# The first two tiles of a gated MLP block by column blocks, with loads reordered, part buffers doubled and the down weight rounded on another engine

## The reference

```
scale = cond @ norm_w.T + 1.0                       # (32, 256)
h = x * (scale[:, None, :] * rsqrt(mean(x*x) + 1e-6))
u = h @ up_w.T                                      # (.., 2048)
val, gate = split(u, 2)
h = val * gelu(gate)
hq = act_quant(h)      # per token: round(h * 127/max|h|) / (127/max|h|)
wq = weight_quant(down_w)   # ternary, by the mean of |down_w|
y = hq @ wq.T
return y + x
```

## Time and profile before

| | before |
|---|---|
| median of 3 runs (lowest to highest) | 429.09 us (429.09 to 429.58) |
| the profiled execution | 429.27 us |
| its span (first to last instruction) | 427.5 us |
| PE busy | 421.1 us, 99% of the span |
| DVE busy | 280.4 us, 66% |
| ACT busy | 186.4 us, 44% |
| POOL busy | 179.9 us, 42% |
| PE's share of the chain that ended last | 94% |

### The profile page before, as it was taken

How to read it: one execution, slowest core, us unless ns; L and a number is a source line. 1 busy time by engine, 2 the same in 40 slices (tenths; PEclk the granted TensorE clock), 3 DMA queues, 4 the chain that set the end, 5 groups by cost and what they waited for, 6 DMA issues and landing times.

```text
span 427.5 us, 7667 instructions
## 1 busy us (share of the span) xinstructions
PE 421.1 (99%) x2081; PEld 337.6 (79%) x2081; DVE 280.4 (66%) x539; ACT 186.4 (44%) x334; POOL 179.9 (42%) x323
## 2 busy tenths in 40 slices
PE   7999999999999999999999999999999999999997
PEld 5688888888887888887888888888878888878786
DVE  4987567556577566576565675565675665765676
ACT  5753444443444444444434444434444434444441
POOL 1564435435345344354344354353453353553520
PEclk9999999999999999999999999999999999999999
DMA  8434443334444334434244433343443344342324
GB/s 281 147 80 115 100 118 103 75 97 123 98 105 115 71 100 106 115 98 107 74 114 98 120 100 77 94 123 98 108 113 73 98 111 109 98 108 75 87 51 124
DMA packets 82024, 45.01 MB, mean 105 GB/s; under 512 B 68256, under 2 KB 68704, under 8 KB 81888
## 3 DMA queue, kind: packets, MB, share of 16 engines
q1 hardware_dynamic: 81584, 44.33, 39.8%
q10 hardware_dynamic: 432, 0.59, 0.4%
HBM read 20.00 MB, written 8.39 MB: 66 GB/s over the span
## 4 chain that ended last, share of the span: by engine, by line
PE 94%; DMA 1%; DVE 1%; SPq 1%; POOL 1%; issue 1%; ACT 0%; DVEq 0%; POOLq 0%
PE p_gate L678 41%; PE p_val L678 41%; PE p_y L698 12%; DMA up_raw<-up_w_t 1%; SPq L219 1%; DVE y_sb L500 0%; PE p_val L650 0%; POOL a_hi L311 0%; POOL scaled L308 0%; PE p_gate L650 0%; DVE q_rounded L526 0%; DVE h L547 0%; PE p_gate L657 0%; POOL a_lo L315 0%; DVE last_max L509 0%
## 5 line engine op out<-in xcount | busy, mean ns | idle before, releaser
L547 DVE SCALAR_TENSOR_TENSOR h<-p_val,rstd,gelu 128x512 f32<-128x512 f32 x128 | 95.3, 746 | 129.9 <-PE p_val L678 129.5
L389 ACT ACTIVATE gelu<-p_gate,rstd 128x512 f32<-128x512 f32 x128 | 87.5, 684 | 149.1 <-PE p_gate L678 139.4
L304 POOL TENSOR_TENSOR mean_sq_eps<-mean_sq,rms_eps 128x1 f32<-128x1 f32 x64 | 12.2, 190 | 224.3 <-PE p_val L678 210.3
L361 ACT ACTIVATE q<-q_rounded 128x1024 bf16<-128x1024 f32 x63 | 66.7, 1058 | 78.2 <-DVE q_rounded L582 78.2
L678 PE MATMUL p_gate<-up_hi,a_lo 128*128 128x512 f32 x248 | 80.6, 406 | 0.6 <-POOL a_lo L315 0.6
L678 PE MATMUL p_val<-up_hi,a_hi 128*128 128x512 f32 x248 | 78.2, 396 | 0.0
L678 PE MATMUL p_val<-up_hi,a_lo 128*128 128x512 f32 x248 | 78.1, 396 | 0.0
L678 PE MATMUL p_val<-up_lo,a_hi 128*128 128x512 f32 x248 | 78.1, 396 | 0.0
L678 PE MATMUL p_gate<-up_lo,a_hi 128*128 128x512 f32 x248 | 78.1, 395 | 0.0
L678 PE MATMUL p_gate<-up_hi,a_hi 128*128 128x512 f32 x248 | 78.1, 395 | 0.0
L568 DVE TENSOR_REDUCE h_max<-h 128x1 f32<-128x1024 f32 x63 | 76.6, 1216 | 1.2
(11 more groups left out here) (74 smaller groups left out, 247.1 us busy)
## 6 DMA issues: line engine op xcount, KB each, us to landing
xt_in<-x_t SPq DMA_DIRECT2D x32, 256.0 KB, 2.8
x_all<-x SPq DMA_DIRECT2D x32, 256.0 KB, 2.9
out<-y_sb SPq DMA_DIRECT2D x31, 256.0 KB, 2.0
up_raw<-up_w_t SPq DMA_DIRECT2D x6, 256.0 KB, 5.4
down_raw<-down_w_t SPq DMA_DIRECT2D x1, 1024.0 KB, 8.0
q_t<-q SPq DMA_TRANSPOSE x63, 3.1
up_raw<-up_w_t ACTq DMA_DIRECT2D x2, 256.0 KB, 3.1
out<-y_sb SPq DMA_DIRECT2D x1, 128.0 KB, 2.0
```

Source lines behind the costliest of these rows:

```text
L304: pool.tensor_tensor(mean_sq_eps[:, j:j + 1], mean_sq[:, j:j + 1], rms_eps[:, :], ALU.add).then_inc(pool_step, 1)
L361: act.activation(q[j % 2][:, :], q_rounded[j % 2][:, :], ACT.Copy, bias=-ROUND).then_inc(q_ready, 1)
L389: act.activation(gelu[c][:, :], p_gate[c][:, :], ACT.Gelu, scale=rstd[:, j:j + 1]).then_inc(gelu_done, 1)
L547: nc.vector.scalar_tensor_tensor(h[s][:, c * W:(c + 1) * W], p_val[c][:, :], rstd[:, j:j + 1], gelu[c][:, :], op0=ALU.mult, op1=ALU.mult). ...
```

## The change

Of the first two tiles, block c = 0 of tile 0, block 0 of tile 1, block 1 of tile 0 and block 1 of tile 1 are made in this order (`early_up`), tile t using the banks `p_gate[t]`, `p_val[t]`. Within a bank the order is a_hi and a_lo for k = 0, a_hi and a_lo for k = 1, then the two up_lo products. All loads go through SP, in a new order. POOL makes tile 1's parts, first of all its tiles; `a_hi` and `a_lo` have four buffers each, and from unit 1 on POOL's work for tile t waits for the values of tile t-3. `scale` is made in two halves in two banks. The down weight: |down_w| later in ACT's queue; the sum over partitions on PE, `ternary(0)` and `ternary(1)` on DVE in tile 2; one pass clips both ways, and the subtraction of `ROUND` with the conversion to bf16 is a copy on ACT (in tile 2, before the square for tile 4). The dummy tile holds ones, and three more dummy matmuls run first.

```diff
-        a_hi = [sb(f"a_hi{i}", [P, KD, P], fp32r) for i in range(2)]
-        a_lo = [sb(f"a_lo{i}", [P, KD, P], fp32r) for i in range(2)]
+        a_hi = [sb(f"a_hi{i}", [P, KD, P], fp32r) for i in range(UNIT)]
+        a_lo = [sb(f"a_lo{i}", [P, KD, P], fp32r) for i in range(UNIT)]
...
+        def early(t, c):
+
+            return t + TPB * c
...
             sp.dma_start(cond_norm_sb[:, :], cond_norm).then_inc(cond_norm_in, 16)
-            load_xt(0, 0)
-            load_up(1)
-            load_up(2)
-            load_x(0, 0)
-            load_up(3)
+            load_up(0, 0)
+            load_xt(0, 0)
+            load_up(0, 1)
+            load_up(1, 0)
+            load_up(1, 1)
+            load_x(0, 0)
+            for c in (2, 3):
+                for k in range(KD):
+                    load_up(c, k)
+            load_xt(0, 1)
             sp.dma_start(down_raw[:, :, :], down_w_t).then_inc(down_in, 16)
-            load_xt(0, 1)
             load_x(0, 1)
...
+            pool.wait_ge(xt_landed[0], 16)
+            product(0, 1)
+            low_part(1, 5)
+            mean(0, 0)
+            root(0, 6)
+            mean(1, 1)
+            root(1, 7)
+            for j in range(TPB, UNIT):
+                if j % TPB == 0:
+                    pool.wait_ge(xt_landed[j // TPB], 16)
+                product(0, j)
+                low_part(j, BEFORE + PER_TILE * (j - 2) + 2)
+                mean(j, j)
+                root(j, BEFORE + PER_TILE * (j - 2) + 3)
+
+            with pool.Fori(1, UNITS) as u:
                 for j in range(UNIT):
...
+                    pool.wait_ge(val_done, NP * (t - 2))
+                    mean(t, j)
+                    product(u, j)
+                    low_part(j, step + 3)
+                    root(j, step + 3)
...
-            for k in range(KD):
-                act.dma_start(up_raw[:, 0, k, :], up_w_t[0, 0, :, k, :]).then_inc(up_in[k], 16)
...
+            for c in range(2):
                 for k in range(KD):
...
+                    high_part(c, k)
+            square(0, 0, True)
+            square(0, 1, True)
+            high_part(2, 0)
+            early_gelu(0, 0)
+            high_part(2, 1)
+            high_part(3, 0)
+            high_part(3, 1)
+            early_gelu(1, 0)
+            early_gelu(0, 1)
+            act.wait_ge(down_in, 16)
+            act.activation(down_tmp[:, :, :], down_raw[:, :, :], ACT.Abs, accum_out=abs_sum[:, :]).then_inc(abs_ready, 1)
+            square(0, 2)
+            early_gelu(1, 1)
+            integers(0, 0, True)
+            square(0, 3)
...
+                    if first and j == TPB:
+
+                        act.wait_ge(ternary_step, 4)
+                        act.activation(down_t[:, :, :], down_tmp[:, :, :], ACT.Copy, bias=-ROUND).then_inc(down_ready, 1)
 
                     if j + 2 < UNIT:
                         square(u, j + 2)
...
-                    nc.vector.tensor_scalar(down_tmp[:, :, :], down_tmp[:, :, :], ROUND, 1.0,
-                                            ALU.subtract, ALU.min).then_inc(ternary_step, 1)
-                if stage == 2:
-
-                    dve.wait_ge(ternary_step, 4)
-                    nc.vector.tensor_scalar(down_t[:, :, :], down_tmp[:, :, :], -1.0, None,
-                                            ALU.max).then_inc(down_ready, 1)
+                    nc.vector.tensor_scalar(down_tmp[:, :, :], down_tmp[:, :, :], ROUND + 1.0, ROUND - 1.0,
+                                            ALU.min, ALU.max).then_inc(ternary_step, 1)
...
+            for c in range(2):
+                for k in range(KD):
+                    low_part(c, k)
+            low_part(2, 0)
+            early_h(0, 0)
+            low_part(2, 1)
+            low_part(3, 0)
+            low_part(3, 1)
+            early_h(1, 0)
+            early_h(0, 1)
+            quantised(0, 0, 0)
+            early_h(1, 1)
+            quantised(0, 1, 1)
+
             def unit(u, first, last=False):
-                for j in range(UNIT):
+                for j in range(TPB if first else 0, UNIT):
...
-                        if first and j == 1 and c == 0:
-                            ternary(1)
+                        if first and j == TPB:
+                            ternary(c)
+                        if first and j == TPB and c == 0:
+                            for done in range(TPB):
+                                rescale(0, done)
...
-            keep_busy(7)
+            keep_busy(10)
...
+            def early_up(t, c):
+
+                n = early(t, c)
+                if t == 1 and c == 0:
+
+                    pe.wait_ge(a_ready, 1)
+                for which, bank, done, read in ((0, p_gate[t], gate_done, gelu_done), (1, p_val[t], val_done, h_done)):
+                    col = 2 * c + which
+                    if c:
+
+                        pe.wait_ge(read, n - 1)
                     for k in range(KD):
...
+                        if t == 0 and c == 0 and which == 0:
+                            pe.wait_ge(a_hi_ready, k + 1)
+                        if t == 0:
+
+                            pe.wait_ge(up_hi_ready, col * KD + k + 1)
+                        nc.tensor.matmul(bank[:, :], a_hi[t][:, k, :], up_hi[:, col, k, :], start=(k == 0), stop=False)
+                        if t == 0 and n == 0 and which == 0 and k == 0:
+                            pe.wait_ge(first_a_ready, 1)
+                        nc.tensor.matmul(bank[:, :], a_lo[t][:, k, :], up_hi[:, col, k, :], start=False, stop=False)
+                    for k in range(KD):
+                        if t == 0:
 
                             pe.wait_ge(up_lo_ready, col * KD + k + 1)
...
+            for c in range(NP):
+                for t in range(TPB):
+                    early_up(t, c)
             unit(0, True)
```

More of the change, by code:

```diff
@@ L329, in tile, with product @@
                                    ALU.pow).then_inc(rstd_ready, 1)
-            def unit(u, first):
-                for j in range(UNIT):
-                    tile(u, j, first)
-            units(pool, unit)
+            def product(u, j):
+                i, half = j // TPB, j % TPB
+                scale = scale_t[:, :, bass.ds(2 * u + i, 1)].to_broadcast([P, KD, P])
+                pool.tensor_tensor(scaled[j % 2][:, :, :], xt_in[i][:, :, half, :], scale,
+                                   ALU.mult).then_inc(pool_step, 1)
+                pool.tensor_tensor(a_hi[j][:, :, :], xt_in[i][:, :, half, :], scale,
+                                   ALU.mult).then_inc(pool_step, 1)
@@ new lines, in low_part @@
+            def low_part(j, step):
+                pool.wait_ge(pool_step, step)
+                pool.tensor_tensor(a_lo[j][:, :, :], scaled[j % 2][:, :, :], a_hi[j][:, :, :].bitcast(fp32),
+                                   ALU.subtract).then_inc(a_ready, 1)
+            pool.wait_ge(xt_landed[0], 16)
[12 more added lines that the diff above has]
+                root(j, BEFORE + PER_TILE * (j - 2) + 3)
@@ L385, in unit @@
                         act.wait_ge(gate_done, NP * t + c + 1)
-                        if not (first and j == 0):
-                            act.wait_ge(h_done, NP * (t - 1) + c + 1)
+                        act.wait_ge(h_done, NP * (t - 1) + c + 1)
                         act.activation(gelu[c][:, :], p_gate[c][:, :], ACT.Gelu,
@@ L656, in up_first, with up @@
                             pe.wait_ge(up_lo_ready, col * KD + k + 1)
-                        last = nc.tensor.matmul(bank[:, :], a_hi[j][:, k, :], up_lo[:, col, k, :],
+                        last = nc.tensor.matmul(bank[:, :], a_hi[t][:, k, :], up_lo[:, col, k, :],
                                                 start=False, stop=(k == KD - 1))
                     last.then_inc(done, 1)
-            def up(u, j, c, first):
-                if first and j < 2:
-                    up_first(j, c)
-                    return
-                s = j % 2
+            def up(u, j, c):
@@ L674, in up @@
                     pe.wait_ge(read, NP * (t - 1) + c + 1)
-                    products = [(a_lo[s], up_hi), (a_hi[s], up_lo), (a_hi[s], up_hi)]
+                    products = [(a_lo[j], up_hi), (a_hi[j], up_lo), (a_hi[j], up_hi)]
                     for n, (a, w) in enumerate(products):
@@ L716, in unit @@
             def unit(u, first, last=False):
-                for j in range(UNIT):
-                    up(u, j, 0, first)
+                for j in range(TPB if first else 0, UNIT):
+                    up(u, j, 0)
                     for n in range(downs_at(j, first, last)):
                         down(u - 1, j + n)
-                    if first and j == 1:
+                    if first and j == TPB:
                         pe.wait_ge(consts_ready, 1)
```

204 lines of the change are left out of this document (83 added, 121 removed).

## The result

The changed kernel took 432.49 us (median of 12 runs, 431.62 to 433.41) against 429.27 for the kernel before (12 runs). The ratio is 1.007, 95% interval 1.0057 to 1.0083: slower by 0.7%, where 429.8 was forecast with 431.2 as the upper end. The profiled execution took 433.07 us, 3.8 more than the one of before; its span is 431.2, 3.7 more. All executions of the changed kernel spread over 1.8 us.

The account below looks back on a forecast made before the run. PE bounds the kernel (busy 421.1 of 427.5 us), so only time before tile 4 could be won. Tile 4 at 18.9 + 12.9 = 31.8, 0.45 later, gave 429.27 + 0.45 = 429.7; predicted 429.8, range 428.1 to 431.2.

Parts of the forecast that it names:

- the sum: Start to tile 4: T 18.9 plus 12.9 puts tile 4 at 31.8 against 31.35, 0.45 us later.
- X: Start of DVE's first a_hi: forecast at 5.3 us, bounds 5.0 and 5.67; 5.67 before.
- VectorE's and GpSimd's contention: In tile 0's first block, DVE and POOL hold each other up: 1.4 us, bounds nothing and 1.97.
- E: End of tile 0's first block: forecast at 10.5 us, range 9.1 to 11.1.
- the page's rule: First block: VectorE and GpSimd share a port pair, two-SBUF-input instructions contend too; E would be about 10.8.
- T: End of tile 1's second block: E + 8.4 = 18.9 us.
- T to tile 4: From the end of tile 1's second block to tile 4's start: 12.9 us, where PE was free after 11.4.
- the stall of 1.55 (1.5): Before tile 4: PE waits 1.5 us, since tile 4's square stands behind the down_t copy in ACT's queue.
- full spacing by the time that matters: First block, likeliest case: PE at full matmul rate in time; tile 4 at 31.2 to 32.0, 429.1 to 429.9; chance 0.38.
- third rival: First block: idle PE stays at 1.2 GHz, eleven matmuls at 0.425, E 12.4; 430.3 to 431.6; chance 0.28 with full exclusion.

Follow-up runs that it names:

- first edit: Changed kernel with the square for tile 4 put ahead of the down-weight copy in ScalarE's queue: 430.88 us, ratio 1.0036 to the kernel before.

## Why the prediction was wrong

**What held.** Nearly all the loss lies before tile 4 and the rest moves with it, up to the 0.45 us at the last stores that go with the single queue and that the sum did not have. X was 5.40 (5.3). VectorE's and GpSimd's contention made a_lo 1.2 us late, and cost 1.38 on up_lo where GpSimd was moved there (1.4). (The 10.8 that the prediction gives for E by the page's rule isn't worked out there; its own terms, 9.1 and the whole 1.97, give the 11.1 of its third rival.) T to tile 4 was 13.12 (12.9), with the stall of 1.55 (1.5) from the copy ahead of the square; the one edit that turns these two round took T to tile 4 back to 11.55 and 1.6 us off the time, so the chain is shown.

**The step that failed** is E = 10.5: it was 12.60. The sum took the first block to end with VectorE's last up_lo, which came at 10.09 where 10.25 was worked out; it left PE's spacing out, "full spacing by the time that matters". PE had eleven matmuls left when a_lo came at 7.74, and at 0.43 us they took 4.9 us. The same spacing took 0.4 us more from the first two matmuls of the next block. These 2.5 us (2.1 in E, 0.4 behind it) are nearly the whole of the 2.7 us between the forecast 31.8 and the measured 34.54 for tile 4 in this execution; 0.2 more are in T to tile 4. Where full spacing was there at 8.4, in the run with fp32r dummies, E was 10.80 and T 19.20, so the rest of the sum was right to 0.3 us. The median of the runs is 0.6 us below this execution; less the 0.45 us of the last stores it stands for a tile 4 at about 34.05 (an estimate: 432.49 less the 398.44 us that the other traces with one queue take from there), so in the typical run the spacing costs about 2.0. The mechanism stands in the prediction as its third rival, with E = 12.4, tile 4 at 32.4 to 33.7 and 430.3 to 431.6. It was given too small a chance, because ten dummy matmuls were taken as evidence against it; without any of them the time is the same (432.66). And even its upper end was 0.9 us short of the result: it stopped at the first block's end, without the 0.4 us behind it, the 0.2 in T to tile 4 and the last stores.

What edits one at a time show: the order of copy and square, 1.6 us; the a_lo that comes late, 1.2 us when GpSimd waits (0.8 when a_hi goes first, not clear of noise); the gaps of PE, 1.5 us when filled. The last two overlap, as both change how much PE has to do at the low level. Together with the two queues they give 3.85 us, more than the whole loss. The rule of the Trainium skill that two SBUF inputs contend (SBUF — State Buffer, Who interferes with whom) was borne out. Its statement that the clock is throttled unless activity releases it (TensorE: Matmul & The Clock Gate, What's actually happening) fits the traces with a hundred dummies ahead of the loads: 0.50 after two gaps, 1.00 with one. It does not by itself explain why a PE that worked from 2.0 us with one wait of 0.64 stayed at the low level to 13.6.

**What stays open** is when the full level comes in a given execution. In the seventeen traces without a hundred dummies ahead of the loads full spacing began between 8.4 and 14.1 us, the latest with the two queues alone. That the moment differs from one execution to the next is shown: the changed kernel and its first edit run the same program up to tile 2, and full spacing began at 13.5 in one and at 10.9 in the other, E was 12.60 and 11.86. The kind of dummies did not settle it, though it may matter: of the four traces with fp32r dummies three are among the earliest (8.4, 8.4 and 8.6) and one is late (13.6), those with bf16 dummies or none go from 8.8, in the kernel before, to 14.1. One trace to a version can't tell, and the medians show no difference. The wide spread of the versions with a late a_lo fits a moment that differs from run to run; that it is the reason is argued and not shown. How the 2.4 us by which E is later than before divide between the level and the gap is settled no better than by the run with fp32r dummies, which fills the gap too: 1.8 of them go with both.

## What to carry to other kernels

In the first microseconds count TensorE's matmuls and not its busy time: matmuls at the lower clock level fill the engine just as well, and the spacing tells. Order the first products so that what is ready goes first and few are left behind the last operand; then the late level costs less. See too that this operand is not held up by another engine: with GpSimd kept behind a_lo the runs spread over 1.0 us instead of 2.2. When a step is moved to another engine's queue, walk through everything behind it in that queue up to what the next tile needs: here one copy of 1.9 us ahead of one small square cost 1.6 us, more than the 1.0 that had been won between the first block and tile 2.

## What the hardware showed that was not expected

- Two waits of 1.62 and 1.50 us with one matmul between them brought a TensorE at full rate back to 0.50 for about 3 us (changed kernel, dummies ahead of the loads); one wait of 1.67 in the kernel before did not.
- A hundred bf16 dummies without a gap did bring full spacing: between 1 and 8 us 48 were started in the changed kernel's trace, where 33 is what 0.213 us apiece allows. Their spacing changed from 0.213 to 0.109 us at 4.6 us, and in the two other traces of that kind at 3.9 and 5.4; two of the three began at the same 1.20 with the same dummies. Seven to ten of them ahead of the real work had no visible effect on the time.
- VectorE's TENSOR_TENSOR and GpSimd's TENSOR_TENSOR, all inputs in SBUF: five of VectorE's took 4.47 instead of 3.09 us, three of GpSimd's 3.01 instead of 1.97, so each lost less than the other's whole time.
- cond_norm, 72 KB, took 2.3 us alone at the head of the queue and 3.2 to 3.5 beside two large loads of another queue, while the last piece of column block 0 came 0.9 us later without that other queue.
- With those two loads on the second queue the last stores, 390 us later, were through some 0.45 us sooner, in ten traces against ten.
